# A four-layer block with two routed feed-forwards: both routing stages written anew

## The reference

```python
x = x + tanh(g_xattn[0]) * retention(norm(x), ctx, ctx)
x = x + tanh(g_ffn[0])   * moe0(norm(x), Wg, W_in, W_out)
x = x + tanh(g_xattn[1]) * attention(norm(x), ctx, ctx, Wq, bq, Wk, bk, Wv, bv, mask, 1)
x = x + tanh(g_ffn[1])   * moe1(norm(x), gate_w, w1, w2)
```

```python
top_vals, top_idx = top_k(softmax(xf @ Wg), 2)
loc = cumsum(onehot(top_idx.T.reshape(-1)), axis=0) - 1      # rank in the expert
keep = loc < 640
gates = top_vals * keep; gates = gates / max(gates.sum(-1), 1e-9)
buf[e, loc] = xf[token]; a, g = split(buf @ W_in[e]); out = (gelu(a) * g) @ W_out[e]
```

## Time and profile before

| | us |
|---|---|
| median of 3 runs (lowest, highest) | 644.98 (643.91, 649.45) |
| the profiled execution, its own time | 642.86 |
| its span in the trace | 641.1 |
| PE busy in it | 546.8 (85%) |
| DVE, ACT, POOL busy | 334.0, 322.5, 233.7 |

### The profile page before, as it was taken

One profiled execution on the slowest core, in us unless ns is written; L12 is line 12 of the kernel. 1 busy time (PEld: TensorE's weight loads), 2 busy tenths in 40 slices (PEclk: granted clock), 3 DMA queues, 4 the chain that ended last, 5 costly groups with the idle time before them and its releaser, 6 DMA issues.

```text
span 641.1 us, 12043 instructions
## 1 busy us (share of the span) xinstructions
PE 546.8 (85%) x3565; PEld 489.0 (76%) x3566; DVE 334.0 (52%) x810; ACT 322.5 (50%) x643; POOL 233.7 (36%) x260
## 2 busy tenths in 40 slices
PE   4897669699999999887777229999999999999991
PEld 2467458699999999855666228898999889889891
DVE  2563953446566665368854764455453544453530
ACT  3495233446666666347774314456454555544540
POOL 3300156335444533355000114354354445354441
PEclk9896787989999999988885559999999999999997
DMA  8923024324534534343014005444452445263221
GB/s 277 373 85 131 2 59 155 114 78 135 162 85 168 172 108 140 107 144 121 33 67 164 1 18 157 108 99 105 107 163 41 128 106 146 38 164 49 33 37 23
DMA packets 51091, 70.59 MB, mean 110 GB/s; under 512 B 6832, under 2 KB 42928, under 8 KB 51056
## 3 DMA queue, kind: packets, MB, share of 16 engines
q1 hardware_dynamic: 40352, 50.04, 23.9%
q0 software_dynamic: 10704, 20.10, 14.1%
HBM read 49.80 MB, written 20.33 MB: 109 GB/s over the span
## 4 chain that ended last, share of the span: by engine, by line
PE 66%; DVE 12%; issue 7%; ACT 5%; DMA 4%; POOL 2%; SPq 1%; DVEq 1%; POOLq 0%; ACTq 0%
PE PA L1392 22%; PE PD L1392 18%; PE PC L1392 7%; PE PD L1267 5%; PE PC L1553 3%; PE PC L1267 3%; DVE ys L937 2%; PE PB L1261 2%; DMA out<-ys,row_o 2%; DVE xs L1071 2%; PE PB L1404 1%; ACT xn L589 1%; DVE wlo L1057 1%; DVE stats L855 1%; PE PB L1535 1%
## 5 line engine op out<-in xcount | busy, mean ns | idle before, releaser
L1392 PE MATMUL PD<-whi,hhi 128*128 128x256 f32 x420 | 122.9, 293 | 0.0
L1392 PE MATMUL PD<-whi,hlo 128*128 128x256 f32 x420 | 118.8, 283 | 0.0
L1392 PE MATMUL PD<-wlo,hhi 128*128 128x256 f32 x420 | 118.8, 283 | 0.0
L543 POOL DMA_INDIRECT out<-ys,row_o x35 | 55.8, 1595 | 104.1 <-DVE ys L1214 103.2
L1392 PEld LDWEIGHTS PD<-wlo,hhi 128*128 128x128 f32 x420 | 80.5, 192 | 0.0
L1392 PEld LDWEIGHTS PD<-whi,hhi 128*128 128x128 f32 x420 | 80.3, 191 | 0.1
L1392 PEld LDWEIGHTS PD<-whi,hlo 128*128 128x128 f32 x420 | 80.3, 191 | 0.0
L813 ACT ACTIVATE hhi<-PC 128x512 fp32r<-128x512 f32 x70 | 38.1, 596 | 67.5 <-PE PC L1553 67.5
L467 POOL DMA_INDIRECT y_rows<-ys,row_y x40 | 41.8, 1045 | 67.2 <-ACT ys L686 65.7
L808 ACT ACTIVATE xT<-PA 128x512 f32<-128x512 f32 x72 | 42.2, 597 | 47.5 <-PE PA L1392 47.2
L1392 PE MATMUL PA<-whi,xhi 128*128 128x512 f32 x144 | 60.3, 419 | 2.6 <-DVE xlo L1057 2.6
(11 more groups left out here) (233 smaller groups left out, 1345.8 us busy)
## 6 DMA issues: line engine op xcount, KB each, us to landing
raw<-w SPq DMA_DIRECT2D x16, 1024.0 KB, 5.6
raw<-L_ffn_W_in SPq DMA_DIRECT2D x8, 1024.0 KB, 5.7
raw<-L_ffn_W_out SPq DMA_DIRECT2D x8, 512.0 KB, 3.5
y_rows<-ys SPq DMA_DIRECT2D x8, 512.0 KB, 8.2
xn_rows<-xn SPq DMA_DIRECT2D x8, 512.0 KB, 3.4
xs<-x SPq DMA_DIRECT2D x4, 512.0 KB, 6.1
cx<-ctx SPq DMA_DIRECT2D x4, 512.0 KB, 6.8
ys<-y_rows SPq DMA_DIRECT2D x4, 512.0 KB, 4.6
```

What stands on the lines that cost most here:

```text
L543: pool.indirect_dma_start(out, bass.IndirectOffsetOnAxis(ap=row_o[:, j:j + 1], axis=0), ys[:, j % 2, :], None, compute_op=ALU.add).then_in ...
L1392: mm = pe.matmul(dst, a[k], b[k], start=(first and k == 0 and a is lhs_hi and b is rhs_hi), stop=(last and k == n - 1 and a is lhs_lo))
```

## The change

What it does, part by part:

1. Top two per quad in layer 0 as well: `choose(0, q)` stands at the end of the pipeline's step q + 3 on DVE and works on the raw logits; the router of each quad signals, and waits for the copy of the logits of the quad before. Softmax and gates of layer 0 leave the front of the stage: they are worked out in `gates0`, on DVE after `hid0(0)`, with ACT's two exponents before `values_out(0)`.
2. Ranks summed in PSUM: DVE makes the running sum `cum` of the one-hots over groups itself (one scan), and two matmuls add into the same bank (`before` is now -1 or 0); the totals come from a third one. Two DVE instructions on 256 numbers go.
3. Shorter indices: rank to int32 directly, `and 127` and `shift 7` give row and tile; `high_slot`, `low_slot` in bf16. A third block of the moving operand (`oha` itself) says whether a slot is used, and row numbers take three instructions (`turned_slots`), the trash rows of the scatter four more after `rows_ready` (`target0_ready`).
4. 16-bit one-hots with the group index innermost, compared with tables of 1280 and 4096 bf16 numbers that ACT writes (`iotas`) in each routing stage. The group product moves from POOL to DVE. `ohb` is written in four parts, and PE starts after the first. PE reads it with a step of 32 numbers, as both operands.
5. Value products and biases: quad 1 moves behind the experts, quad 0's values behind `invert(0)`; PE's first `xt0` waits for the evacuation of values 0. `value_bias(1)` on POOL moves to before `share(0)`, `pad(1)` on DVE to before `split1`.
6. ACT: splits of expert 0's weights before `part_part(0)`; tables for Gelu and Silu are loaded by one-element activations before the work that needs them. SP: the weights of expert 1 wait for the first three `xt0`.
7. Layer 1's end: `xt1` and `hid1(0, 0)` on PE, `xt1(0, 0)` on ACT stand before the wait for `tab_ready`; `split1(wout)` of ACT after `part_part(1)`; `gate_values(1)` before `ohb`.

The core of the diff:

```diff
+                if 0 <= t - 3:
+                    choose(0, t - 3)
+            choose(0, NQ - 1)
...
+                link(dve.tensor_tensor_scan(flat(cum[:, :, :]), c("reset"), flat(oh[:, :, :]), 0.0, ALU.mult, ALU.add))
+                dve.sem_inc(cum_ready, 1)
...
+                    link(dve.tensor_reduce(smi[:, 0, :], loc[:, :, :].rearrange("p e g -> p g e"), AX.X, ALU.add))
+                link(dve.tensor_scalar(smi[:, 1, :], smi[:, 0, :], P - 1, None, ALU.bitwise_and))
+                link(dve.tensor_scalar(smi[:, 2, :], smi[:, 0, :], 7, None, ALU.arith_shift_right))
...
+            def turned_slots(layer):
+                dve.wait_ge(map_done, layer + 1)
+                part, group = (PD[:, 0, 128 + n * NA:128 + (n + 1) * NA] for n in range(2))
+                link(dve.tensor_copy(inv[:, 0, :], group))
+                link(dve.scalar_tensor_tensor(row_y[:, :], inv[:, 0, :], float(P), part, ALU.mult, ALU.add))
+                link(dve.tensor_scalar(row_x[:, :], row_y[:, :], T - 1, None, ALU.bitwise_and))
+                dve.sem_inc(rows_ready, 1)
...
+            def maps(layer):
+                dve.wait_ge(iota_ready, layer + 1)
+                link(dve.tensor_copy(low_slot[:, :], smi[:, 1, :]))
+                dve.tensor_tensor(oha, high_slot[:, :].unsqueeze(1).broadcast_to([P, NA, NG]), iota_a, ALU.is_equal)\
+                    .then_inc(oha_ready, 1)
+                dve.wait_ge(oha_ready, layer + 1)
+                dve.tensor_tensor(by_group, oha, group_b.unsqueeze(1).broadcast_to([P, NA, NG]), ALU.mult)\
+                    .then_inc(group_ready, 1)
                 if layer == 1:
                     gate_values(1, NQ - 1, NQ)
+                for n in range(MAP_PARTS):
+                    at = slice(n * NG // MAP_PARTS, (n + 1) * NG // MAP_PARTS)
+                    dve.tensor_tensor(ohb[:, :, at],
+                                      low_slot[:, at].unsqueeze(1).broadcast_to([P, P, NG // MAP_PARTS]),
+                                      iota_n[:, :, at], ALU.is_equal).then_inc(map_ready, 1)
...
+            hid0(0, first=True)        # DVE
+            gates0()
+            dve.wait_ge(mask_in, 16)
+            pad(0)
             out0(0)
...
-                pe.matmul(PD[:, 1, 0:E * NG], before, flat(oh[:, :, :]), start=True, stop=True)
-                pe.matmul(PD[:, 1, E * NG:2 * E * NG], ones_b, flat(oh[:, :, :]), start=True, stop=True)\
-                    .then_inc(rank_done, 1)
+                pe.matmul(PD[:, 1, 0:E * NG], before, flat(oh[:, :, :]), start=True, stop=False)
+                pe.wait_ge(cum_ready, layer + 1)
+                pe.matmul(PD[:, 0, 256:256 + E], ones_b, cum[:, :, NG - 1], start=True, stop=True)\
+                    .then_inc(totals_done, 1)
+                pe.matmul(PD[:, 1, 0:E * NG], ones_b, flat(cum[:, :, :]), start=False, stop=True).then_inc(rank_done, 1)
...
                 for g in range(NG):
-                    mm = pe.matmul(PD[:, 0, 128:128 + 2 * NA], ohb[:, g, :], rhs_a[:, g, :], start=(g == 0),
+                    if g % (NG // MAP_PARTS) == 0:
+                        pe.wait_ge(map_ready, layer * MAP_PARTS + g // (NG // MAP_PARTS) + 1)
+                    mm = pe.matmul(PD[:, 0, 128:128 + MAP_BLOCKS * NA], ohb[:, :, g], rhs_a[:, :, g], start=(g == 0),
                                    stop=(g == NG - 1))
...
             context("cT again", 0)
             pe.wait_ge(cb_ready, 1)
             ranks(0)
+            biases(0)
+            invert(0)
             values(0)
-            context("cT again", 1)
-            invert(0)
-            values(1)
...
-            pe.wait_ge(evac_done, EV1["bias", 1])
+            pe.wait_ge(evac_done, EV1["v", 0])
...
             pe.wait_ge(hid0_used, E * STEPS0 + 2)
-            for q in range(2, NQ):
+            for q in range(1, NQ):
                 context("cT again", q)
                 values(q)
+                biases(q)
```

More of the change, by code:

```diff
@@ L69 @@
 CF_W = _at
-CB = {"before": (0, P), "ones": (P, 2 * P)}
+CB = {"before": (0, P), "ones": (P, 2 * P), "group": (2 * P, 2 * P + NG)}
+CB_W = 2 * P + NG
+MAP_PARTS = 4
+MAP_BLOCKS = 3
 def constants():
@@ L90, in constants @@
     put("eps", LN_EPS)
-    put("group1", np.arange(1, NG + 1)[None, :])
+    put("group", np.arange(NG)[None, :])
     put("ones", 1.0)
-    put("before", r[:, None] < r[None, :])
+    put("before", (r[:, None] < r[None, :]) - 1.0)
     put("iota", r[None, :])
@@ L201, in build @@
         ident, decay = c("ident"), c("decay")
-        before, ones_b = (cb[:, a:b] for a, b in (CB["before"], CB["ones"]))
+        before, ones_b, group_b = (cb[:, a:b] for a, b in (CB["before"], CB["ones"], CB["group"]))
         def wout_half(k):
@@ L492, in _ @@
             gather0(1)
-            for q in range(2):
-                value_bias(q)
+            value_bias(0)
+            pool.wait_ge(target0_ready, 1)
             for e in range(E):
@@ L515, in _ @@
             pool.wait_ge(gates_ready, 1)
+            value_bias(1)
             for q in range(NQ):
@@ L868, in coefs, with best_two, choose @@
                 dve.sem_inc(coef_ready, 1)
+            def best_two(src, tiles):
+                for b in tiles:
+                    ins = dve.max(top[:, b, :], src[:, b, :])
+                link(ins)
+                for b in tiles:
+                    ins = dve.max_index(topi[:, b, :], top[:, b, :], src[:, b, :])
+                link(ins)
+            logits = PD[:, 0, 0:NB * E].rearrange("p (b e) -> p b e", e=E)
+            def choose(layer, q):
+                dve.wait_ge(lg_done, layer * NQ + q + 1)
+                quad = slice(q * QB, (q + 1) * QB)
+                link(dve.tensor_copy(lg[:, quad, :], logits[:, quad, :]))
+                dve.sem_inc(lg_used, 1)
+                best_two(lg, range(q * QB, (q + 1) * QB))
             for t in range(NQ + 2):
@@ new lines, in _ @@
+            one_hots(0)
+            dve.wait_ge(rank_done, 1)
+            pick()
+            link(dve.tensor_scalar(sm[:, 1, :], smi[:, 0, :], float(CAP), float(64), ALU.is_ge, ALU.mult))
+            link(dve.scalar_tensor_tensor(sm[:, 2, :], eidx[:, :], float(CT), smi[:, 2, :], ALU.mult, ALU.add))
+            link(dve.tensor_tensor(high_slot[:, :], sm[:, 1, :], sm[:, 2, :], ALU.add))
+            maps(0)
+            dve.wait_ge(zero_out, 16 * K * NQ)
+            link(dve.tensor_tensor(lg[:, :, :], lg[:, :, :], top[:, :, 0:1].broadcast_to([P, NB, E]), ALU.subtract))
@@ new lines, in _ @@
+            link(dve.tensor_tensor(rr[:, 0, :], top[:, :, 1], top[:, :, 0], ALU.subtract))
+            dve.sem_inc(e_arg, 1)
+            turned_slots(0)
+            dve.wait_ge(totals_done, 1)
+            link(dve.tensor_scalar(full[:, :], totals, float(CAP - P), None, ALU.is_gt))
+            link(dve.tensor_tensor(inv[:, 2, :], row_y[:, :], c("trash"), ALU.subtract))
+            link(dve.tensor_tensor(inv[:, 3, :], inv[:, 2, :], real, ALU.mult))
+            link(dve.tensor_tensor(row_y[:, :], inv[:, 3, :], c("trash"), ALU.add))
@@ L996, in pad @@
                     .then_inc(pad_ready, 1)
-            dve.wait_ge(mask_in, 16)
-            for q in range(2):
-                pad(q)
             def win0(e, k):
```

258 lines of the change are left out of this document (114 added, 144 removed).

## The result

The changed kernel takes 651.43 us (median of 4 runs, 650.88 to 652.05) against 644.79 for the kernel before on the same chip: ratio 1.0131, 95% interval 1.0098 to 1.0163. It is slower by 1.3%. The forecast was 636.5, faster by 1.3%; the time lies outside the range, 5.4 above its upper end. The profiled execution took 651.5, with a span of 649.7 (641.1 before).

The account below looks back on a forecast made before the run. PE was taken to carry the span outside four gaps, three of which the change touches. The terms 9.7 - 2.6 - 5.5 + 6.4 gave 8.0 earlier than 642.86, 634.9; with 2.1 for the timed runs' median, 636.5 was named, range 628 to 646.

Parts of the forecast that it names:

- What bounds the kernel: Whole kernel: PE carries the span; DVE or ACT changes count only inside its four gaps, whose shifts pass to the end.
- 16-bit comparisons and DVE's standstill behind POOL: Routing stages: comparisons at two numbers a cycle, 4.1 for `ohb`; its 6.61 held a stall behind POOL, saved too.
- The 32 matmuls: Inversion in both routing stages: 3.4 in all with strided reads, dear end 6.8; cheap end taken.
- rival (a): Both routing stages: strided reads take twice as long, each loses 3.4, gain 1.2, about 643.5; chance 0.17.
- The first stage: Layer 0 routing: first gather at 78.9, first expert matmul near 88.4, 9.7 earlier, bounds 6 and 11.
- Rival (d): First stage bound more by ACT's queue, or products merely change place: 9.7 becomes 5, whole 3.3, 641.5; chance 0.14.
- `gates0` and `pad(0)`: DVE between `hid0(0)` and expert 1's splits: 3.6 of work holds up PE's third turn, 2.6 lost (0 to 3.6).
- The pause: A new pause like the 6.42 between experts 0 and 1, elsewhere: 6 us either way, not in the sum.
- The middle: Between experts and attention: quad 1's block makes the first turn 7.3 late, some given back, 5.5 late (3.5 to 7.5).
- moving is no saving: Between experts and attention: moving quad 1's products only moves them; cover there is used up, a block of 8.4 added.
- Rival (c): Between experts and attention: all three blocks at half clock, 42 in place of 19.6, about 651; chance 0.06.
- The second stage: Layer 1 routing: first gather 5.7 earlier, first expert matmul near 377.1 against 383.47, 6.4 earlier (5.5 to 7.5).

Follow-up runs that it names:

- w = 1: Changed kernel with both one-hots laid group by group, so PE reads without gaps and DVE's source is one number held per row: R 1.0048.
- the test by itself: 18 idle matmuls ahead of the experts' loop against 18 behind it, on the changed kernel with paired one-hots and gates moved: 633.60 against 641.66.
- before_move: Kernel before with only quad 1's products moved behind the experts, and 30 idle matmuls ahead of the inversion: R 1.0128.
- pad18_ahead: Changed kernel with paired one-hots, `gates0` and `pad(0)` ahead of `hid0(0)`, and 18 idle matmuls ahead of the inversion: 633.60, R 0.9786.
- best: Changed kernel with paired one-hots, gates ahead of `hid0(0)`, quad 1's products back ahead of the experts, its biases behind two pairs of turns: R 0.9826.
- pad18_again: The kernel of pad18_ahead run once more, for comparison on one chip: 633.13, R 0.9809.

## Why the prediction was wrong

*What bounds the kernel*: right. What was gained or lost in the gaps came through to the end, and 1.5 more was lost in the experts of layer 1.

*16-bit comparisons and DVE's standstill behind POOL*: right, 0.83, 0.82 and 2.49 against 0.82, 0.82 and 4 x 0.62; w = 1 shows the dear end, 1.49, 1.49 and 4.62.

*The 32 matmuls*: the step that failed first. Its bounds were 3.4 and 6.8, and I took the cheap end "since at half clock PE asks for half as much". Measured 7.12 and 7.10, beyond even the dear end. PE does ask for less at half clock, but the wide step has its own pace, 218 to 220 ns a matmul at either clock, and half clock covered only the 100 that a matmul takes then anyway. This took 3.7 from each stage. With that put right the sum is 8.0 - 7.4 = 0.6: rival (a), which had 0.17. The only price without a row on which both stages hung, and with a stated rule against it, should have had more.

*The first stage*: 9.7 became 5.3; 3.7 of the difference is the matmuls. They began 1.3 earlier than forecast (72.98 against 74.3), but from the first gather to the first expert it took 11.6 rather than 9.5. Of these 2.1, 1.3 is POOL: from its first gather to its fourth it needed 5.2 rather than 3.9, since the second and the third took 1.74 and 1.42 while DVE made `wlo`; the other 0.8 lies between the fourth gather and the expert. Rival (d) had named the size, 9.7 becoming 5, but ACT's queue, its first cause, was not behind it.

*`gates0` and `pad(0)`*: 2.6 forecast, 2.0 measured; mechanism right.

*The pause*: named as what could make it wrong, "6 us either way", and given no term or chance of its own. The sum put it at nothing. It cost 6.6 in the profile (4.5 of pause, 2.1 of slower matmuls behind it) and 8.1 in the test by itself. This, with the reads, turns the forecast around: -8.0 + 7.4 + 6.6 is +6.0, and the smaller misses of the table make the rest of +8.7.

*The middle*: 5.5 forecast (3.5 to 7.5), 6.4 measured from the experts' end to the last router. The move's price was right, the turn 6.7 late where 7.3 was forecast; that 1.8 of it would be given back was not, it was 0.3 (from the turn to the last router 64.5, before 64.8). And "moving is no saving" stood beside a gain ahead of the experts that I counted in full as 9.7. before_move has no gain there.

*Rival (c)* named 651, and 651.4 was measured; that is chance. It had all three blocks at half clock, 42 together; they took 26.4, and only the first had its products at a lower clock (5.22, the others 3.72).

*The second stage*: 6.4 became 1.7. From the logits to the first expert I had 21.1 and it took 25.8; 3.7 of the 4.7 is the matmuls, 0.5 the way from the last table entry to the first expert (2.5 rather than 2.0), the rest small steps.

*The arithmetic*: 642.86 - 8.0 + 2.1 is 637.0, not 636.5, and rival (a) by the same working is 643.8, not 643.5; neither changes the account.

With its two faults mended the change does what was forecast and somewhat more: pad18_ahead keeps all its parts, with runs of 2, the gates moved, and the pause absent, and has R 0.9786, 2.1% faster. That is not the forecast come true, since the shorter tables and the moved gates are gains that it did not have.

## What to carry to other kernels

Lay out what PE multiplies so that neighbours in a read lie 4 bytes apart and not 16 or more; a comparison on DVE still runs at its faster pace when its innermost runs hold 2. When a change adds or removes code ahead of a loop, look at the loop's first pass and its exit for a pause in "issue" with a packet on the instruction queue beside it, and try a few idle instructions before blaming the change. And a small DVE product on the way to the next stage should not stand beside a tensor instruction of POOL. Compare across chips by ratios, expectations too.

## What the runs showed of the hardware that I had not expected

- Matmuls of 120 bf16 columns follow each other after 100 ns at half clock (1.2 GHz) and 54 at full with a step of 4 bytes, and after 218 to 220 with 16 or 64 (16 seen at both clocks, 64 with both operands at half clock). It is the multiplied side that pays (204 ns alone), not the weights (100 alone).
- Eighteen idle matmuls ahead of the loop, rather than behind it, are worth 1.2% here.
- DVE and POOL can hold each other up: beside the 4.55 of `best`, the gathers of 1.74 and 1.42 in the changed kernel, where 0.95 is usual.
- The last router of layer 0 ended between 60.1 and 63.3 in the profiles of the versions of the changed kernel, which hardly differ up to there: some 3 us that are settled before the part under study. One kernel run twice, pad18_ahead and pad18_again, had 61.8 and 63.1.
